# Attention scores computed a second time with keys on partitions instead of turning the probabilities; queries, keys and values made ahead of logits and output projection

## The reference

```python
q = Q @ Wq + bq; k = K @ Wk + bk; v = V @ Wv + bv      # layer 0: 16 heads of 8 channels
# layer 1 uses one 8 x 8 weight per projection for all 16 heads, and a mask over the keys
scores = q @ k.T * scale                                # 64 x 64 per batch and head; scale 8**-0.5, then 128**-0.5
attn = softmax(scores) @ v
x = x + tanh(gate) * (attn @ Wo + bo)
# layer 0 feed-forward: router over 8 experts, the two best per token, 128 -> 512 -> 128
# layer 1 feed-forward: 4 gated experts, 128 -> 256 -> 128
```

## Time and profile before

| what | us |
|---|---|
| median of 3 runs | 1433.82 |
| lowest, highest | 1426.07, 1438.8 |
| span of the profiled execution, first to last instruction | 1173.7 |
| busy: TensorE, VectorE, ScalarE, GpSimd | 1095.9, 902.1, 715.9, 543.8 |

### The profile page before, as it was taken

How to read it: one execution, slowest core, us unless ns; L and a number is a source line. 1 busy time by engine, 2 the same in 40 slices (tenths; PEclk the granted TensorE clock), 3 DMA queues, 4 the chain that set the end, 5 groups by cost and what they waited for, 6 DMA issues and landing times.

```text
span 1173.7 us, 39887 instructions
## 1 busy us (share of the span) xinstructions
PE 1095.9 (93%) x13589; PEld 930.7 (79%) x13589; DVE 902.1 (77%) x3189; ACT 715.9 (61%) x1565; POOL 543.8 (46%) x699
## 2 busy tenths in 40 slices
PE   6899999999984899999999799999999979999998
PEld 4777777777762899999999577777777768999997
DVE  4778878889887454554543699999999979988886
ACT  4777778777760555555555577777777744444443
POOL 2112565556757334344443866666666421222230
PEclk7999999999996899999999899999999999999999
DMA  7223311111202333333333222222222100000000
GB/s 199 71 79 92 92 56 54 54 55 55 68 29 83 90 94 95 93 96 96 94 95 84 56 50 52 49 48 48 51 50 50 24 2 10 27 18 26 18 18 28
DMA packets 116781, 71.88 MB, mean 61 GB/s; under 512 B 51737, under 2 KB 105241, under 8 KB 116633
## 3 DMA queue, kind: packets, MB, share of 16 engines
q1 hardware_dynamic: 108440, 53.13, 16.8%
q0 software_dynamic: 8192, 16.79, 4.8%
HBM read 45.88 MB, written 22.94 MB: 59 GB/s over the span
## 4 chain that ended last, share of the span: by engine, by line
PE 69%; DVE 8%; ACT 7%; issue 7%; POOL 4%; SPq 2%; DMA 2%; DVEq 0%; ACTq 0%; POOLq 0%
PE ps_m L1741 11%; PE ps_m L1518 8%; PE ps_p L1506 7%; PE ps_s L1468 5%; PE ps_p L1622 5%; PE ps_m L1622 4%; PE ps_s L1478 4%; PE ps_s L1727 3%; PE ps_s L1728 3%; PE ps_s L1729 3%; ACT Kbd L749 3%; PE ps_m L1494 2%; ACT Pr L739 2%; PE ps_s L1610 2%; PE ps_s L1611 2%
## 5 line engine op out<-in xcount | busy, mean ns | idle before, releaser
L970 DVE TENSOR_REDUCE mx<-ps_s 128x8 f32<-128x512 f32 x256 | 168.7, 680 | 36.7 <-PE ps_s L1468 36.3
L1518 PEld LDWEIGHTS ps_m<-Vbd,PT 128*64 128x64 f32 x4096 | 137.8, 138 | 48.4 <-issue 42.8
L709 ACT ACTIVATE PT<-ps_p 128x512 f32<-128x512 f32 x256 | 152.7, 597 | 27.0 <-PE ps_p L1506 24.8
L1518 PE MATMUL ps_m<-Vbd,PT 128*64 128x18 f32 x4096 | 158.2, 213 | 0.2 <-ACT PT L709 0.2
L786 ACT ACTIVATE Kbd<-ps_s,c 128x512 f32<-128x512 f32 x128 | 87.3, 688 | 114.5 <-PE ps_s L1612 114.5
L1506 PE MATMUL ps_p<-cst,Pr 128*128 128x128 f32 x1024 | 155.2, 280 | 0.4 <-DVE orow L1246 0.4
L572 POOL TENSOR_TENSOR spare<-spare 1x1 f32<-1x1 f32 x99 | 21.1, 213 | 285.4 <-DVE b1s L1329 146.0
L648 POOL DMA_INDIRECT w1a<-louts,gi x128 | 125.5, 980 | 38.6 <-issue 29.5
L1741 PE MATMUL ps_m<-xn3T 128*128 128x128 f32 x1136 | 138.0, 275 | 0.2 <-ACT xn3T L851 0.2
L1741 PEld LDWEIGHTS ps_m<-xn3T 128*128 128x128 f32 x1136 | 132.7, 192 | 0.4 <-issue 0.4
L851 ACT ACTIVATE xn3T<-ps_s,b1s 128x256 f32<-128x256 f32 x284 | 111.2, 474 | 26.1 <-PE ps_s L1729 26.0
(11 more groups left out here) (219 smaller groups left out, 2695.8 us busy)
## 6 DMA issues: line engine op xcount, KB each, us to landing
xn3T<-lists SPq DMA_DIRECT2D x71, 128.0 KB, 2.1
louts<-xn3T SPq DMA_DIRECT2D x71, 128.0 KB, 1.9
ctxg<-in_ctxT SPq DMA_DIRECT2D x32, 256.0 KB
Kbd<-in_ctxT SPq DMA_DIRECT2D x512, 8.0 KB
out<-x SPq DMA_DIRECT2D x16, 256.0 KB, 2.3
w1a<-in_L_ffn_W SPq DMA_DIRECT2D x8, 256.0 KB, 3.3
w2a<-in_L_ffn_W SPq DMA_DIRECT2D x8, 256.0 KB, 4.0
Pr<-in_ctxT SPq DMA_DIRECT2D x16, 128.0 KB, 2.4
```

The lines of the kernel that those rows point to most:

```text
L709: return nc.scalar.activation(dst, src, ACT.Copy)
L970: V.tensor_reduce(mx[g.par][:, q, :], per_key(ps_s[:, q, :]), AX, ALU.max).then_inc(max_done, 1)
L1518: ins = mm((bank7, bank6)[pr][S * b:S * b + S, VW * j:VW * (j + 1)], PT[c][:, P * i + S * b:P * i + S * b + S], Vbd[g.par][:, 2 * pr + b, ...
```

## The change

The probabilities are no longer turned. The scores are computed twice from the same rows `qk` (`scores(g, half)`): once with queries on partitions (banks 0 and 1 of `ps_s`), only to find the maximum, and once with keys on partitions (banks 2 and 3), with the negated maximum added as one more contraction row. The exponential of the second kind is what `probs_by_values` needs. Both are matmuls of 8 to 10 contraction rows and 64 x 64 results, 128 of them per group; `probs_by_values` becomes 128 matmuls of 64 contraction rows, 32 output partitions and 9 columns. The number of matmul instructions in the program goes from 6651 to 18108.

The maxima travel: VectorE `maximum` (two per group, 128x1024), TensorE `maxima_turned`, ScalarE `maxima_out`, SyncE `maxima_in` into row 8 or 9 of `qk`. Queries (and in layer 0 keys) are copied by ScalarE (`queries_staged`) and laid out by four DMAs of SyncE (`queries_in`); in layer 1 keys come from `keys` in DRAM, stored in layer 0, and the mask is one more row (`masks_in`).

Gone: `less_maximum`, `mxh`, `mxl`, the two subtractions, `Kbd` with its four copies, `probs_turned` with its four copies, the spread values `Vbd`. Exponentials are two of 128x1024 in place of four of 128x512. The layer norms of layer 1 go from VectorE to ScalarE, with a small `means_scaled` on VectorE.

The pipeline is one step longer at either end (g = -5 to 36). On GpSimd `inverse_deviations` now stands first in the step, ahead of `rows_plus_constant` (`xc`):

```diff
-                if have(-1) and not (g.layer == 0 and g.k > LATE_SUMS):
-                    rows_plus_constant(g.plus(-1))
+                if have(-3) or have(3):
+                    inverse_deviations(g)
+                if have(-2) and not (g.layer == 0 and g.k > LATE_SUMS):
+                    rows_plus_constant(g.plus(-2))
...
-                if have(-2) or have(2):
-                    inverse_deviations(g)
...
-                    elif have(-8):
-                        scatter(g.plus(-8), (0, 1))
+                    elif have(-9):
+                        scatter(g.plus(-9), (0, 1))
                 else:
-                    if have(4):
-                        gather(g.plus(4))
...
+                    if have(5):
+                        gather(g.plus(5))
```

The step of VectorE in layer 1, after the change, is `statistics_in` 3, `moments` 3, `combine` 4, `gate_logits` -4, `residual` -3, `statistics_mid` -3, `moments` -3, `maximum` half 0, and the rest. The step of SyncE:

```diff
             def step(g):
-                if g.plus(2).real() and (g.layer or g.k >= 0):
-                    load_ctx(g.plus(2))
+                if g.plus(-1).real():
+                    maxima_in(g.plus(-1))
+                if g.plus(1).real():
+                    queries_in(g.plus(1), 0)
+                    if g.layer == 1:
+                        masks_in(g.plus(1))
+                    queries_in(g.plus(1), 1)
```

```diff
+                for u in range(2):
+                    for h in range(HB):
+                        for i in range(2):
+                            token = slice(P * u + S * i, P * u + S * i + S)
+                            side = slice(S * i, S * i + S)
+                            col = slice(S * (2 * h + u), S * (2 * h + u) + S)
...
+                                for r in range(2):
+                                    q = 2 * half + r
+                                    rows = slice(32 * q, 32 * q + ROWS + own.layer)
+                                    ins = mm(ps_s[side, r, col], src[rows, h, 0, token], src[rows, h, 1, token],
+                                             start=True, stop=True, skip_group_check=True)
...
+                                for r in range(2):
+                                    q = 2 * other + r
+                                    rows = slice(32 * q, 32 * q + ROWS + 1 + turned.layer)
+                                    ins = mm(ps_s[side, 2 + r, col], src[rows, h, 1, token], src[rows, h, 0, token],
+                                             start=True, stop=True, skip_group_check=True)
```

More of the change, by code:

```diff
@@ L1538, in values @@
[L1538 to L1541 removed]
+                if g.plus(3).real():
+                    pe.wait_ge(xnT_ready, g.plus(3).count(1, 1))
+                else:
+                    wait(pe, v_ready, g.count(1, 0))
+                for u in range(2):
+                    ins = mm(side_bank[:, P * u:P * u + P], ctxg[g.k % KEYS][:, P * u:P * u + P], wv[0][:, :],
+                             start=True, stop=True)
```

881 lines of the change are left out of this document (430 added, 451 removed).

## The result

The changed kernel takes 1929.2 us (median of 4 runs, 1925.3 to 1931.9); the kernel before took 1436.3 in the same job (1426.1 to 1450.4). The ratio is 1.346, 95% interval 1.340 to 1.351. The prediction said slower, 1510, with a range of 1470 to 1605: the direction is right, the size is a long way off. First the page of the changed kernel: span, busy time, granted clock in 40 slices, two groups of matmuls, and the queue that brings instructions.

The account below looks back on a forecast made before the run. The prediction took layer 1's loop through GpSimd's gathers, closed over one step, as the bound: span 1173.7, less 0.3 for layer 0, plus 76.3 for layer 1, is 1249.7; with 260.1 outside the span, 1510 us, range 1470 to 1605.

Parts of the forecast that it names:

- the pricing of the small matmuls: TensorE in layer 0: `probs_by_values` 2.2 us, with the scores' second half, hidden by 4.4 us of residual to normalise.
- the base: Span 1173.7 us; the median 1433.8 is 260.1 more, taken to lie outside the span and added at the end.
- the ring: Layer 1: the loop through moments, gathers and `combine` closes over one step, 12.0 us instead of 9.05; main term, +76.3.
- 9 ns: TensorE's price per record of a small matmul with 64 columns; half of the scores, 128 records, 1.15 us.
- small matmuls at twice my price: Rival, chance 0.17: 17 ns a record on TensorE, 13 us a step in layer 0, about 1605 us in all.
- The clock: TensorE's granted clock, read as full in the middle of layer 1 and kept so in pricing its matmuls.
- In layer 0, forecast at -0.3: Layer 0: 9.5 us a step against 10.3, offset by the later start; last scatter at 380.6, so nothing gained.
- The start: Layer 0: `queries_in(0)` stands behind SyncE's held queue, so the first maximum comes at about 36, not 17.08.

Follow-up runs that it names:

- the new profile: The kernel before, with no edit, profiled once more: time 1436.2 us, span 1434.4.
- the kernel before with the ring put in: The kernel before with `combine` of group g+3 moved ahead of residual and moments of the leaving group in layer 1: 1449.5 us against 1423.4, ratio 1.019.
- lean: The changed kernel with 64 bfloat16 products of probabilities and values a group, and bfloat16 scores for the maximum: 1570.3 us, ratio 1.109.
- lean without them: The changed kernel with those bfloat16 products and scores, and memsets in place of GpSimd's gathers in layer 1: 1449.6 us.

## Why the prediction was wrong

The step that failed is the pricing of the small matmuls: "`probs_by_values`, 256 records, 2.2", with the second half of the scores "hidden by 4.4 us of it", at a clock held at 1.00 and with no idle time in a stream of records. In its place the runs showed a product of about 9 us on TensorE's path and the clock at 0.50 in layer 1. Two further steps were wrong, the base and the ring.

**The base.** "These 260.1 at the end", the first step of the sum, failed. The 260.1 between span and median were no time outside the span but the difference between an unusual execution and the usual ones: the new profile has 110 of it in the steps of layer 0, 127 in those of layer 1 and 22 between them. The usual kernel before has steps of 14.5 and 13.8, not 10.3 and 9.05. 64 steps that are some 4 us longer make most of 260, and this could have been asked of the number. A span with the rest added gives the median of the old kernel by construction, so the sum could not show the error. It even made the forecast better by luck: against the span the sum said 1249.7, and the changed kernel's is 1930.1, 680 more; the 260.1 cover a good third of that.

**The small matmuls.** The term "9 ns" a record was right for as long as instructions were there (204 records in 1.87 us); half of the scores, priced at 1.15, took 1.6 in step 1 at the full clock (47.70 to 49.32) and 2.1 at 1.2 GHz. What failed is that the price of a record was taken as the price of a stream. `probs_by_values` was priced at 2.2 and hidden; it takes 5.9 in step 3 (75.77 to 81.62) and about 9 in the middle of layer 1, on the path, with TensorE idle for 5.3 of it and busy for 4.2 in the mean of steps 2 to 27. The rival "small matmuls at twice my price" (1605) was the nearest case, with the wrong reason; nothing in it was a pause of whole microseconds. What the Trainium skill, "TensorEngine Tiling (Array Packing)", section "Performance Considerations", says of some 60 cycles a matmul, by estimate 25 ns a record at the full clock, is not borne out: there the bursts went at 9 ns. At the lower clock, where it would be an estimated 50, they went at 11 to 16, and at 29 to 35 for 64 output partitions.

**The clock.** I held it at 1.00. It is 0.50 in layer 1 and 0.52 to 0.57 in layer 0. The work of TensorE other than `probs_by_values` takes some 10 us of a step of layer 1 at this level; by estimate it would be about 6 at the other (the two halves of the scores 4.2 and, from the 1.6 of step 1, 3.2; the large matmuls 5.7 and about half of it). This was no rival of mine at all.

**The ring.** It is closed in the order of the program, but no run shows it as a bound. Its 12.0 a step would lie under steps of 20.6; the sign that was to show it, VectorE idle about 5 us ahead of each `combine` until the rows land, came five times in all. In the kernel before with the ring put in, it came five times too. Where +76.3 was forecast for the ring, layer 1 took +199 for other reasons (from the first to the last first maximum, 606.8 against 407.4 in the new profile of the kernel before). In layer 0, forecast at -0.3, the same stretch takes 637.2 for 428.8, +208.

**The start.** First maximum forecast at 36, found at 36.89. It costs 20, near the 19 forecast. The rest of the 496 us between the two spans: 41 between the last first maximum of layer 0 and the first of layer 1, and 27 at the end.

How the step of layer 1 divides, by the runs: 20.6 to 16.1 by records (lean), to 11.9 by gathers (lean without them), and 2.5 more to the 9.4 of the kernel before without gathers. The shares hang on the order: with the gathers taken first they are 1.8 and the records 7.0. I put the last 2.5, and a share of the first, down to the low clock and the 2.0 us a step that TensorE still idles in the lean kernel without gathers; no run brought the clock of the changed kernel back, so its share is not measured by itself.

## What to carry over

Before adding a span and "the rest" to a sum, see whether the rest can be the steps: divide it by their number. Count the instructions of a step as well as their time, since TensorE can use them up faster than they arrive; trading a few large matmuls for hundreds of small ones costs in records, in pauses and in clock. And look where GpSimd issues indirect DMAs: in two parts they cost this kernel far less than in one.

## What the hardware showed

- When TensorE asks for instructions densely, it pauses at places that lie a multiple of 256 of them apart: 1.8 to 3.3 us in the rows shown, ended 2.2 to 2.8 behind the start of a 16 KB block's arrival. With some 36 records a us instead of 52, idle time without a wait was 0.3 us a step instead of 5.8.
- In the usual executions, where GpSimd issued four indirect DMAs in a row (4.9 us), a result of TensorE reached VectorE 4.75 us behind its record instead of 1.5; with plain DMAs of SyncE for as many bytes the kernel was 9.1% faster (ratio 0.909). In the execution with the span of 1173.7 the same DMAs delayed nothing.
- 256 small records a step brought the granted clock from 2.4 to 1.2 GHz for 6 to 7 us of each step of 17; seven large matmuls in their place did not.
- One program has shown spans of 1173.7 and 1434.4 us with the same instructions.
